# Rotated queries transposed one iteration later in a four-stage fused kernel

## Chip, cores and metric

The kernel runs on one core of a Trainium2 chip. The metric is the time of one execution on the device in microseconds (us), the median of the runs.

## What is computed

Four residual layers over x of 64 batches x 64 tokens x 512 features (float32), each with its own choice of weights per batch or per block:

```
x = x + L0(x)   # einsum('bsi,bio->bso', x, W[id]) + b[id]     16 experts, one per batch
x = x + L1(x)   # x @ W.T + low-rank adapter (A[idx], Bm[idx]) * scaling[idx], 8 adapters
x = x + L2(x)   # attention with a paged key/value cache:
                #   q, k, v = x @ Wq.T, x @ Wk.T, x @ Wv.T     8 query heads, 4 key/value heads of 64
                #   q, k = rope(rms(q)), rope(rms(k))
                #   new k, v are written into blocks; each query sees a window of 256 keys
                #   out = softmax(q k / 16) v @ Wo.T
x = x + L3(x)   # einsum('bct,bcd->bdt', x, weights[subject]) + bias[subject]
```

## The kernel before

The program is written engine by engine, with semaphores between them. Two batches (128 tokens) form a pair; there are NP = 32 pairs. **Phase one** goes over the pairs and does L0, L1, the projections of L2 and the rotation of queries and keys; the results (x2, the rotated queries, new key/value rows) go to DRAM. **Phase two** goes over the 64 batches and does attention, the output projection and L3. The change lies in phase one alone.

Each engine has its own function `phase_one(k, j, s)` for iteration k. The helper `loop` runs k = 0 to 3 written out, k = 4 to 29 in a hardware loop of two iterations a turn (s = 0 for even k, s = 1 for odd k), and the last ones written out. What an engine does in iteration k belongs to several pairs, since the work of a pair is spread over iterations. `on(k, lag, NP)` says whether the pair k - lag exists. In iteration k

- PE (TensorE) does, in this order: the experts of pair k (`experts`, L602), the transpositions of x2 of pair k-1 (`transpose_x2`, L612), the transpositions of rotated queries of pair k-2 (`transpose_queries`, L677), the transpositions of x1 of pair k (L706), the projections of pair k-1 to queries, keys and values (`project_inputs`, L654 to L666, with the adapter L623 in between), the dense part of L1 for pair k (L728, L732);
- ACT (ScalarE) copies and rounds x2 (x2t_hi, L919), copies the transposed queries into q_t (`copy_queries`, L905), copies x1 (L926, L927), and later stores q_t to DRAM (`store_queries`, L910) and squares the projections (L963, L964);
- DVE (VectorE) adds the experts' result to x (x1, L1200), forms the low parts (L1205, L1234), the sums for the norm (ss, L1257, L1259), the products of the rotation (L1265 to L1268) and x2 (L1276);
- POOL (GpSimd) does the rotation of pair k-2: the power for the norm (rms, L471), the sum (L475), the scaled rotated queries (q_rot, L480), the same for the keys (L482, L485), and the tables (L494) and x plus bias (L461) of later pairs;
- SP issues the loads, two iterations ahead, and stores.

`q_rot` and `q_t` have two buffers, one for even and one for odd pairs. POOL overwrites a buffer of q_rot once its old pair has been transposed (semaphore t3_done); PE waits for POOL (rot_q_ready) and for ACT's copy out of its PSUM bank (qt_ready). On each engine the order of the code is the order of execution; a wait holds all that stands behind it on that engine.

In the last iterations the order differs. In k = 31 (NP-1) three transpositions of index rows stand ahead of L677. In k = 32 (NP) PE has no experts; it transposes x2 of pair 31, projects it (L639), transposes the queries of pair 30 behind that, and keeps its clock up with transpositions whose result isn't used (`keep_warm`, L579). In k = 33 the queries of pair 31, which DVE has rotated (L1183), are transposed.

Of the kernel before, what the change touches and what calls it, by code (L numbers as in the profile page):

```python
# [13 lines left out]
P = 128  # L14
# [45 lines left out]
def build(nc, a):  # L60

    ctx = ExitStack()
    with ctx:
# [195 lines left out]
        def wait(eng, semaphore, value):  # L259

            if not isinstance(value, int) or value > 0:
                eng.wait_ge(semaphore, value)
# [312 lines left out]
        def _(pe):  # L575
# [90 lines left out]
                            last = nc.tensor.matmul(ps_out[:, :], x2t_hi[:, c, :], wqkv_lo[:, c, n0:n0 + D], start=False, stop=(c == DC - 1))  # L666
                    last.then_inc(qkv_done, 1)

            def transpose_queries(k, s):

                if isinstance(k, int) and k == NP + 1:
                    pe.wait_ge(q_last, 1)
                else:
                    pe.wait_ge(rot_q_ready, k - 1)
                wait(pe, qt_ready, k - 2)
                for c in range(DC):
                    last = nc.tensor.transpose(ps_t3[:, c * P:(c + 1) * P], q_rot[:, s, c * P:(c + 1) * P], ident[:, :])  # L677
                last.then_inc(t3_done, 1)

            def phase_one(k, j, s):  # L680
                r = 1 - s
                if isinstance(k, int) and k == 1:
                    transpose_x2(k, r)
                    project_inputs(k, s)
                    experts(k, j, s)
                else:
                    if on(k, 0, NP):
                        experts(k, j, s)
                    if on(k, 1, NP):
                        transpose_x2(k, r)  # L690
                if isinstance(k, int) and k == NP - 1:
# [3 lines left out]
                    for c in range(2):  # L695
                        nc.tensor.transpose(ps_la[:, (1 + c) * P:(2 + c) * P], rows[0][:, c:WIN:PAIR], ident[:, :])
                    nc.tensor.transpose(ps_la[:, P + WIN:], rows[0][:, WIN:WIN + P], ident[:, :]).then_inc(idx_t, 1)
                if on(k, 2, NP) and not (isinstance(k, int) and k == NP):
                    transpose_queries(k, s)
                if on(k, 0, NP):  # L700
                    pe.wait_ge(x1_ready, k + 1)
                    wait(pe, x1hi_ready, k)
# [7 lines left out]
                if not (isinstance(k, int) and k == 1):  # L710
                    project_inputs(k, s)
                if isinstance(k, int) and k == NP:
                    transpose_queries(k, s)
                    pe.wait_ge(x1_ready, NP)
                    keep_warm(WARM_Q)
                if on(k, 0, NP):

                    if isinstance(k, int) and k < 2:
                        adapt_down(k, s)
                    wait(pe, x2_ready, k)  # L720
                    if isinstance(k, int) and k == 0:
                        pe.wait_ge(w_hi_ready, 1)
                        pe.wait_ge(w1_lo_ready, 1)
                    pe.wait_ge(x1hi_ready, k + 1)
                    pe.wait_ge(x1lo_ready, k + 1)
                    for x_part, w_part in ((x1t_hi, w1_hi), (x1t_hi, w1_lo), (x1t_lo, w1_hi)):
                        for c in range(DC):
                            nc.tensor.matmul(ps_l1[:, :], x_part[:, c, :], w_part[:, c, :],  # L728
                                             start=(c == 0 and x_part is x1t_hi and w_part is w1_hi), stop=False)
                    pe.wait_ge(xa_ready, k + 1)  # L730
                    pe.wait_ge(pb_ready, k + 1)
                    nc.tensor.matmul(ps_l1[:, :], xa_parts[:, :], pair_b_parts[:, s, :], start=False, stop=True).then_inc(h_done, 1)  # L732
# [135 lines left out]
        def _(act):  # L868
# [29 lines left out]
            for k in range(2):  # L898
                take_adapters(k, k, copy=False)

            def copy_queries(k, j, s):

                act.wait_ge(t3_done, k - 1)
                wait(act, st_q[s], 16 * j - 16)
                nc.scalar.activation(q_t[:, s, :, :, :], ps_t3[:, :].rearrange("p (c h t) -> p h c t", c=DC, h=2),  # L905
                                     ACT.Copy).then_inc(qt_ready, 1)

            def store_queries(k, s):
                act.wait_ge(qt_ready, k - 1)
                act.dma_start(q_dram[bass.ds(k - 2, 1)].rearrange("o p n -> (o p) n"),  # L910
                              q_t[:, s, :, :, :].rearrange("p h c t -> p (h c t)")).then_inc(st_q[s], 16)

            def phase_one(k, j, s):
                r = 1 - s
                if on(k, 1, NP):

                    act.wait_ge(t2_done, k)
                    wait(act, qkv_done, k - 1)
                    nc.scalar.activation(x2t_hi[:, :, :].rearrange("p c t -> p (c t)"), ps_t2[:, :], ACT.Copy).then_inc(x2hi_ready, 1)  # L919
                if on(k, 2, NP) and not (isinstance(k, int) and k == NP):  # L920
                    copy_queries(k, j, s)
                if on(k, 0, NP):

                    act.wait_ge(t1_done, k + 1)
# [18 lines left out]
                if isinstance(k, int) and k == 0:  # L943
                    act.wait_ge(ld_wkv, 2 * 16)
                    nc.scalar.activation(wqkv_hi[:, :, D:], wqkv_stage[:, :, D:], ACT.Copy).then_inc(w_hi_ready, 1)
                if on(k, 2, NP) and not (isinstance(k, int) and k == NP):
                    store_queries(k, s)
                if isinstance(k, int) and k == NP:

                    act.wait_ge(kv_done, 1)  # L950
# [3 lines left out]
                    nc.scalar.activation(kv_out[:, r, 256:512], ps_kv[:, 256:512], ACT.Copy).then_inc(v_ready, 1)  # L954
                    act.wait_ge(qkv_done, k)
                    nc.scalar.activation(sq[:, 0:8, :].rearrange("p g d -> p (g d)"), ps_q[:, :], ACT.Square).then_inc(sqv_ready, 1)
                    copy_queries(k, j, s)
                    store_queries(k, s)
                elif on(k, 1, NP):

                    act.wait_ge(qkv_done, k)
# [474 lines left out]
```

## Time and profile before

| | |
|---|---|
| runs | 950.08, 950.8, 954.0 us; median 950.8 |
| profiled execution | span 948.6 us (its time outside the span isn't recorded) |
| mean granted clock of PE | 0.982 |
| busy | PE 96%, PE weight loads 70%, DVE 69%, POOL 55%, ACT 47% of the span |
| phase one | up to about 500 us: 32 iterations, most of them of 14.6 to 14.7 us |
| turn to phase two | about 500 to 530 us |
| phase two | from there to the end |

Times in the rows are in us from the start of the span, durations of single instructions too. PE's matmuls are pipelined: a group's busy time holds the way of the last one through the array, so the start of one group and the start of the next tell more than its end. PEld is the weight load that belongs to a matmul or transposition.

### The profile page before, as it was taken

What the parts mean: (1) busy time and instruction counts of PE and PEld (TensorE: products, weight loads), DVE (VectorE), ACT (ScalarE), POOL (GpSimd) and SP (SyncE); (2) the same over time, 40 slices, a digit from 0 to 9 for tenths busy, and PEclk for the clock granted to TensorE, in tenths of its full rate; (3) what the DMA queues carried; (4) which work ended last, traced back from release to release, by engine and by line L of the source; (5) the groups of instructions that cost most, each with busy time, mean ns of one, the idle gap of its engine ahead of it and who ended that gap; (6) DMA issues with size and microseconds to landing.
All of it is one profiled execution on the core that took longest, in us unless ns stands there. A gap on an engine that the chain in (4) does not pass through costs nothing.

```text
span 948.6 us, 23332 instructions
## 1 busy us (share of the span) xinstructions
PE 907.5 (96%) x6477; PEld 660.8 (70%) x6477; DVE 651.1 (69%) x1853; ACT 444.3 (47%) x1190; POOL 522.3 (55%) x502
## 2 busy tenths in 40 slices
PE   5789999999999999999997899999999999999997
PEld 3456666766666667666676777877777887787785
DVE  5345545667768774556754678777878877888875
ACT  2333333333333333333322566666666666666663
POOL 2136455464564657855556666566565665656530
PEclk9799999999999999999998799999999999999999
DMA  9978988778788787887844566666666676567741
GB/s 295 265 230 282 330 308 290 252 261 289 247 282 276 244 291 255 271 295 247 284 159 152 183 188 203 199 210 186 198 197 212 200 225 203 181 209 212 221 135 46
DMA packets 100413, 218.51 MB, mean 230 GB/s; under 512 B 30187, under 2 KB 36168, under 8 KB 92178
## 3 DMA queue, kind: packets, MB, share of 16 engines
q1 hardware_dynamic: 66290, 145.27, 47.0%
q0 software_dynamic: 25088, 57.74, 20.5%
q10 hardware_dynamic: 8992, 15.00, 4.9%
q8 instruction: 18, 0.29, 0.1%
q14 instruction: 25, 0.20, 0.1%
HBM read 210.39 MB, written 33.86 MB: 257 GB/s over the span
## 4 chain that ended last, share of the span: by engine, by line
PE 51%; POOL 18%; issue 15%; DMA 7%; SPq 4%; DVE 2%; ACT 1%; ACTq 1%; POOLq 0%; DVEq 0%
PE banks L823 9%; PE banks L775 9%; PE banks L811 7%; PE banks L798 6%; POOL rms L471 5%; DMA ring<-in_rope 5%; PE banks L752 4%; PE banks L859 3%; POOL ring L475 3%; POOL x_in L461 3%; PE banks L816 3%; POOL q_rot L480 2%; PE banks L753 1%; PE banks L791 1%; POOL ring L482 1%
## 5 line engine op out<-in xcount | busy, mean ns | idle before, releaser
L561 POOL DMA_INDIRECT ring<-new_rows,idx x128 | 129.4, 1011 | 82.5 <-PE banks L775 40.3
L471 POOL TENSOR_TENSOR rms<-ss,neg_half 128x12 f32<-128x12 f32 x31 | 70.8, 2284 | 185.4 <-DVE ss L1259 185.4
L992 ACT ACTIVATE big<-big,neg_max 128x320 f32<-128x320 f32 x256 | 141.4, 554 | 3.1 <-DVE neg_max L1317 2.7
L1317 DVE CUSTOM_DVE_ANT_0 big<-banks,mask 128x320 f32<-128x320 f32 x256 | 114.6, 486 | 27.4 <-PE banks L775 26.0
L602 PE MATMUL banks<-ring 128*64 128x512 f32 x512 | 117.8, 601 | 0.9 <-DMA ring<-in_w 0.9
L982 ACT ACTIVATE kt<-banks 128x384 f32<-128x384 f32 x128 | 61.8, 483 | 97.5 <-PE banks L753 97.5
L775 PE MATMUL banks<-kt,q_in 64*128 64x128 f32 (+2 forms) x768 | 88.6, 364 | 1.3 <-ACT kt L982 1.3
L550 POOL DMA_INDIRECT ring<-new_rows,idx x64 | 61.7, 965 | 47.0 <-PE banks L798 42.7
L1354 DVE TENSOR_SCALAR big<-big,recip 128x320 f32<-128x320 f32 x256 | 85.5, 396 | 2.3
L775 PEld LDWEIGHTS banks<-kt,q_in 64*128 64x128 f32 x768 | 74.4, 189 | 14.4 <-issue 8.4
L811 PEld LDWEIGHTS banks<-pt,ring 128*64 128x64 f32 x1024 | 55.4, 136 | 38.1 <-DVE pt L1299 25.4
L602 PEld LDWEIGHTS banks<-ring 128*64 128x64 f32 x512 | 34.1, 137 | 67.6 <-issue 66.8
L919 ACT ACTIVATE x2t_hi<-banks 128x512 fp32r<-128x512 f32 x32 | 19.1, 598 | 128.0 <-PE banks L612 128.0
L514 POOL DMA_INDIRECT ring<-in_kvrows,idx x64 | 61.2, 956 | 28.8 <-issue 13.5
L811 PE MATMUL banks<-pt,ring 128*64 128x128 f32 x1024 | 70.0, 278 | 2.7 <-DVE pt L1299 2.3
L664 PE MATMUL banks<-wqkv_hi,x2t_lo 128*128 128x512 f32 x248 | 70.4, 405 | 0.0
L798 PE MATMUL banks<-ident,big 128*128 128x128 f32 x512 | 67.4, 275 | 0.4 <-DVE ot_lo L1306 0.4
L654 PE MATMUL banks<-wqkv_hi,x2t_hi 128*128 128x512 f32 x248 | 66.6, 412 | 0.7 <-ACT x2t_hi L919 0.7
L666 PE MATMUL banks<-wqkv_lo,x2t_hi 128*128 128x512 f32 x248 | 66.6, 390 | 0.0
L1234 DVE TENSOR_TENSOR x1t_lo<-x1t,x1t_hi 128x512 fp32r<-128x512 f32 x32 | 40.3, 1258 | 35.9 <-ACT x1t L927 35.9
L1200 DVE TENSOR_TENSOR x<-banks,x_in 128x512 f32<-128x512 f32 x32 | 22.1, 691 | 55.6 <-PE banks L602 50.9
L798 PEld LDWEIGHTS banks<-ident,big 128*128 128x128 f32 x512 | 58.5, 142 | 1.0 <-DVE ot_lo L1306 0.9
(177 smaller groups left out, 1989.0 us busy)
## 6 DMA issues: line engine op xcount, KB each, us to landing
ring<-in_w SPq DMA_DIRECT2D x62, 1024.0 KB, 7.5
ring<-in_xt SPq DMA_DIRECT2D x32, 256.0 KB, 2.7
x_in<-in_x SPq DMA_DIRECT2D x32, 256.0 KB, 5.8
bias_in<-in_b SPq DMA_DIRECT2D x64, 128.0 KB, 6.4
x_dram<-x SPq DMA_DIRECT2D x32, 256.0 KB, 6.9
q_dram<-q_t ACTq DMA_DIRECT2D x32, 256.0 KB, 5.7
new_rows<-kv_out SPq DMA_DIRECT2D x32, 256.0 KB, 6.7
q_in<-q_dram SPq DMA_DIRECT2D x32, 256.0 KB, 2.7
```

The source lines that it names most:

```text
L471: nc.gpsimd.tensor_tensor(rms[:, s, :], ss[:, s, :], neg_half[:, :], ALU.pow).then_inc(rms_ready, 1)
L561: pool.indirect_dma_start(out=kv[:, s, c, :], out_offset=None, in_=new_rows, in_offset=bass.IndirectOffsetOnAxis(ap=idx[:, b, 1 + c:2 + c] ...
L602: last = nc.tensor.matmul(ps_l0[T * h:T * h + T, :], xt[:, s, c, T * h:T * h + T], w0[:, 2 * s + h, c * D:(c + 1) * D], start=(c == 0), st ...
L654: nc.tensor.matmul(ps_out[:, :], x2t_hi[:, c, :], wqkv_hi[:, c, n0:n0 + D], start=(c == 0), stop=False)
L664: nc.tensor.matmul(ps_out[:, :], x2t_lo[:, c, :], wqkv_hi[:, c, n0:n0 + D], start=False, stop=False)
L775: return nc.tensor.matmul(banks[:, S0[g] + n0:S0[g] + n1], q_in[r0:r0 + HD, s % 4, g // 2, :], kt[r0:r0 + HD, s % 2, g // 2, k0 + n0:k0 + ...
L798: last = nc.tensor.transpose(ps_pt[p][:, (q * 2 + c) * P:(q * 2 + c + 1) * P], prob[:, r % 2, (5 * p + 3 * q + c) * P:(5 * p + 3 * q + c + ...
L811: nc.tensor.matmul(ps_o[p][HD * q:HD * q + HD, :], kv[:, r, c, v0:v0 + HD], pt[:, p, PLACE[2 * p + q] % 2, c, :], start=(c == 0), stop=Fal ...
L823: last = nc.tensor.matmul(out[:, n0:n1], o_part[:, pair_s, c, :], w_part[:, c, n0:n1], start=(c == 0 and n == 0), stop=(c == DC - 1 and n ...
L992: nc.scalar.activation(prob[:, s % 2, PLACE[g] * NK:(PLACE[g] + 1) * NK], sm[:, s % 2, g, :], ACT.Exp, bias=neg_max[:, s % 2, g:g + 1], sc ...
L1317: V.tensor_tensor_reduce(sm[:, s % 2, g, :], ps_s[g], mask[:, s % 2, k0:k0 + NK], 1.0, 3.0e38, ALU.add, ALU.min, accum_out=neg_max[:, s % ...
L1354: V.tensor_scalar(own_row, own_row, recip[:, s % 2, g:g + 1], None, ALU.mult).then_inc(prob_ready, 1)
```

## The change

The rotated queries of pair k-3, not k-2, are transposed in iteration k, at the same place of PE's order. The copies and stores on ACT move along. The functions now take the pair and its buffer as arguments. Where the pairs run out, in k = 32, the queries of pair 29 are transposed ahead of x2 and copied ahead of x2t_hi; pairs 30 and 31 stay where they were.

```diff
-            def transpose_queries(k, s):
-                if isinstance(k, int) and k == NP + 1:
+            def transpose_queries(pair, t):
+                if is_last(pair):
                     pe.wait_ge(q_last, 1)
                 else:
-                    pe.wait_ge(rot_q_ready, k - 1)
-                wait(pe, qt_ready, k - 2)
+                    pe.wait_ge(rot_q_ready, pair + 1)
+                wait(pe, qt_ready, pair)
                 for c in range(DC):
-                    last = nc.tensor.transpose(ps_t3[:, c * P:(c + 1) * P], q_rot[:, s, c * P:(c + 1) * P], ident[:, :])
+                    last = nc.tensor.transpose(ps_t3[:, c * P:(c + 1) * P], q_rot[:, t, c * P:(c + 1) * P], ident[:, :])
...
                     if on(k, 0, NP):
                         experts(k, j, s)
+                    if isinstance(k, int) and k == NP:
+                        transpose_queries(NP - 3, r)
                     if on(k, 1, NP):
                         transpose_x2(k, r)
...
-                if on(k, 2, NP) and not (isinstance(k, int) and k == NP):
-                    transpose_queries(k, s)
+                if on(k, 3, NP) and on(k, 0, NP):
+                    transpose_queries(k - 3, r)
...
                 if isinstance(k, int) and k == NP:
-                    transpose_queries(k, s)
+                    transpose_queries(NP - 2, s)
                     pe.wait_ge(x1_ready, NP)
                     keep_warm(WARM_Q)
+                if isinstance(k, int) and k == NP + 1:
+                    transpose_queries(NP - 1, s)
...
-            def copy_queries(k, j, s):
-                act.wait_ge(t3_done, k - 1)
-                wait(act, st_q[s], 16 * j - 16)
+            def copy_queries(pair, half, t):
+                act.wait_ge(t3_done, pair + 1)
+                wait(act, st_q[t], 16 * half)
...
+                if isinstance(k, int) and k == NP:
+                    copy_queries(NP - 3, NP // 2 - 2, r)
                 if on(k, 1, NP):
                     act.wait_ge(t2_done, k)
...
-                if on(k, 2, NP) and not (isinstance(k, int) and k == NP):
-                    copy_queries(k, j, s)
+                if on(k, 3, NP) and on(k, 0, NP):
+                    copy_queries(k - 3, j - 2 + s, r)
+                if isinstance(k, int) and k == NP + 1:
+                    copy_queries(NP - 1, NP // 2 - 1, s)
...
-                if on(k, 2, NP) and not (isinstance(k, int) and k == NP):
-                    store_queries(k, s)
+                if on(k, 3, NP) and on(k, 0, NP):
+                    store_queries(k - 3, r)
+                if isinstance(k, int) and k == NP:
+                    store_queries(NP - 3, r)
+                if isinstance(k, int) and k == NP + 1:
+                    store_queries(NP - 1, s)
```

The order on PE in the even half of the loop, from the experts to the projections; before (`ident` is the unit matrix that a transposition multiplies with, a name in brackets is the semaphore waited for):

```order
L612 MATMUL banks<-ident,x2 128x128 [waits x2lo_ready]
L612 MATMUL banks<-ident,x2 128x128 x3
L262 REGISTER_ALU [waits rot_q_ready]
L677 MATMUL banks<-ident,q_rot 128x128 [waits qt_ready]
L677 MATMUL banks<-ident,q_rot 128x128 x3
L701 REGISTER_ALU
L706 MATMUL banks<-ident,x1 128x128 [waits x1hi_ready,x1_ready]
L706 MATMUL banks<-ident,x1 128x128 x3
L654 MATMUL banks<-wqkv_hi,x2t_hi 128x512 [waits sqv_ready,ab_ready,x2hi_ready]
```

The same place with the change:

```order
L612 MATMUL banks<-ident,x2 128x128 [waits x2lo_ready]
L612 MATMUL banks<-ident,x2 128x128 x3
L674 REGISTER_ALU
L262 REGISTER_ALU [waits rot_q_ready]
L677 MATMUL banks<-ident,q_rot 128x128 [waits qt_ready]
L677 MATMUL banks<-ident,q_rot 128x128 x3
L703 REGISTER_ALU
L708 MATMUL banks<-ident,x1 128x128 [waits x1hi_ready,x1_ready]
L708 MATMUL banks<-ident,x1 128x128 x3
L654 MATMUL banks<-wqkv_hi,x2t_hi 128x512 [waits sqv_ready,ab_ready,x2hi_ready]
```

Nothing changes its place; one register instruction (L674) is added ahead of L677, and what L677 reads and the count that it waits for are those of the pair before. In the odd half, and in the iterations that are written out, no register instruction is added there.

ACT in k = 32 and behind it, before:

```order
L919 ACTIVATE x2t_hi<-banks 128x512 [waits qkv_done,t2_done]
L952 ACTIVATE sq<-banks 128x256 [waits ss_ready,kv_done]
L954 ACTIVATE kv_out<-banks 128x256 [waits st_kv1]
L956 ACTIVATE sq<-banks 128x512 [waits qkv_done]
L905 ACTIVATE q_t<-banks 128x512 [waits st_q0,t3_done]
L910 DMA q_dram<-q_t 128x512 [waits qt_ready]
```

The same with the change:

```order
L909 ACTIVATE q_t<-banks 128x512 [waits st_q1,t3_done]
L925 ACTIVATE x2t_hi<-banks 128x512 [waits qkv_done,t2_done]
L914 DMA q_dram<-q_t 128x512 [waits qt_ready]
L964 ACTIVATE sq<-banks 128x256 [waits ss_ready,kv_done]
L966 ACTIVATE kv_out<-banks 128x256 [waits st_kv1]
L968 ACTIVATE sq<-banks 128x512 [waits qkv_done]
L909 ACTIVATE q_t<-banks 128x512 [waits st_q0,t3_done]
L914 DMA q_dram<-q_t 128x512 [waits qt_ready]
```

A copy (L909) is added ahead of x2t_hi, and its store (L914) behind it. On PE four transpositions are added ahead of L612 of this iteration.

## Rows read from the trace of the kernel before

**Rows 1.** The page, the chain that ended last: share of the span by engine.

```profile
PE 51%; POOL 18%; issue 15%; DMA 7%; SPq 4%; DVE 2%; ACT 1%; ACTq 1%; POOLq 0%; DVEq 0%
```

**Rows 2.** Waits of PE's weight loads: who waited for whom: us, times, longest.

```profile
PEld banks L677 <- POOL q_rot L480: 5.5, 15, 0.8
PEld banks L677 <- issue: 4.9, 13, 0.5
```

**Rows 3.** Waits of PE's matmuls.

```profile
PE banks L602 <- DMA ring<-in_w: 0.9, 2, 0.5
```

**Rows 4.** Waits of POOL.

```profile
POOL rms L471 <- DVE ss L1259: 185.4, 31, 13.3
```

**Rows 5.** Stretch k = 3 to 29: length, busy time by engine, granted clock, DMA share.

```profile
76.32:457.26 380.94, 377.70 (x2108) 250.75 (x2107) 246.26 (x517) 134.18 (x286) 219.95 (x196) 1.00 0.85 276
```

**Rows 6.** Timeline of k = 15: start, us, engine, line, operation [idle before <- releaser].

```profile
252.02 1.04 POOL L480 TENSOR_TENSOR q_rot<-ring,rms 128x512 f32<-128x512 f32 x1
252.26 0.42 PEld L612 LDWEIGHTS banks<-ident,x 128*128 128x128 f32 x4 [0.81 <-issue]
...
252.38 0.69 DVE L1200 TENSOR_TENSOR x<-banks,x_in 128x512 f32<-128x512 f32 x1 [1.33 <-PE banks L602]
252.95 0.60 ACT L919 ACTIVATE x2t_hi<-banks 128x512 fp32r<-128x512 f32 x1 [3.92 <-PE banks L612]
...
253.11 0.42 PEld L677 LDWEIGHTS banks<-ident,q_rot 128*128 128x128 f32 x4 [0.44 <-POOL q_rot L480]
...
253.50 0.47 PEld L706 LDWEIGHTS banks<-ident,x 128*128 128x128 f32 x4
...
253.94 1.69 PEld L654 LDWEIGHTS banks<-wqkv_hi,x2t_hi 128*128 128x128 f32 x8
```

**Rows 7.** Timeline of k = 16.

```profile
264.93 0.68 DVE L1276 TENSOR_TENSOR x<-banks,x 128x512 f32<-128x512 f32 x1
...
266.57 1.04 POOL L480 TENSOR_TENSOR q_rot<-ring,rms 128x512 f32<-128x512 f32 x1
266.98 0.42 PEld L612 LDWEIGHTS banks<-ident,x 128*128 128x128 f32 x4 [0.81 <-issue]
...
267.74 0.42 PEld L677 LDWEIGHTS banks<-ident,q_rot 128*128 128x128 f32 x4 [0.33 <-issue]
...
267.76 0.60 ACT L919 ACTIVATE x2t_hi<-banks 128x512 fp32r<-128x512 f32 x1 [3.97 <-PE banks L612]
...
268.56 1.70 PEld L654 LDWEIGHTS banks<-wqkv_hi,x2t_hi 128*128 128x128 f32 x8
```

**Rows 8.** Timeline, L612 and L654 of k = 3, 29 and 30.

```profile
76.32 0.42 PEld L612 LDWEIGHTS banks<-ident,x 128*128 128x128 f32 x4 [0.81 <-issue]
...
77.84 0.77 PEld L654 LDWEIGHTS banks<-wqkv_hi,x2t_hi 128*128 128x128 f32 x4
...
457.26 0.42 PEld L612 LDWEIGHTS banks<-ident,x 128*128 128x128 f32 x4 [0.81 <-DVE x L1276]
...
459.29 0.30 PEld L654 LDWEIGHTS banks<-wqkv_hi,x2t_hi 128*128 128x128 f32 x2
...
472.34 0.42 PEld L612 LDWEIGHTS banks<-ident,x 128*128 128x128 f32 x4 [0.81 <-issue]
...
473.85 0.53 PEld L654 LDWEIGHTS banks<-wqkv_hi,x2t_hi 128*128 128x128 f32 x3
```

**Rows 9.** Timeline of k = 32, the turn to phase two.

```profile
500.24 0.65 PE L612 MATMUL banks<-ident,x 128*128 128x128 f32 x4 [2.20 <-DVE x L1276]
500.93 0.60 ACT L919 ACTIVATE x2t_hi<-banks 128x512 fp32r<-128x512 f32 x1 [4.65 <-PE banks L612]
...
501.58 1.79 PE L639 MATMUL banks<-wqkv_hi,x2t_hi 128*128 128x512 f32 x4 [0.69 <-ACT x2t_hi L919]
```

**Rows 10.** Two stretches of the turn: columns as in rows 5.

```profile
501.50:505.00 3.50, 3.42 (x9) 2.70 (x10) 0.69 (x1) 0.03 (x1) 2.04 (x3) 0.56 0.27 103
...
513.26:533.00 19.74, 16.18 (x82) 13.63 (x82) 8.64 (x30) 6.64 (x19) 14.43 (x15) 0.65 0.59 176
```

More of the change, by code:

```diff
@@ L899, in _, with store_queries @@
                 take_adapters(k, k, copy=False)
-            def copy_queries(k, j, s):
-                act.wait_ge(t3_done, k - 1)
-                wait(act, st_q[s], 16 * j - 16)
-                nc.scalar.activation(q_t[:, s, :, :, :], ps_t3[:, :].rearrange("p (c h t) -> p h c t", c=DC, h=2),
+            def copy_queries(pair, half, t):
+                act.wait_ge(t3_done, pair + 1)
+                wait(act, st_q[t], 16 * half)
+                nc.scalar.activation(q_t[:, t, :, :, :], ps_t3[:, :].rearrange("p (c h t) -> p h c t", c=DC, h=2),
                                      ACT.Copy).then_inc(qt_ready, 1)
[L908 to L911, printed above, removed]
+            def store_queries(pair, t):
+                act.wait_ge(qt_ready, pair + 1)
+                act.dma_start(q_dram[bass.ds(pair, 1)].rearrange("o p n -> (o p) n"),
+                              q_t[:, t, :, :, :].rearrange("p h c t -> p (h c t)")).then_inc(st_q[t], 16)
             def phase_one(k, j, s):
                 r = 1 - s
+                if isinstance(k, int) and k == NP:
+                    copy_queries(NP - 3, NP // 2 - 2, r)
                 if on(k, 1, NP):
@@ L956, in phase_one @@
                     nc.scalar.activation(sq[:, 0:8, :].rearrange("p g d -> p (g d)"), ps_q[:, :], ACT.Square).then_inc(sqv_ready, 1)
-                    copy_queries(k, j, s)
-                    store_queries(k, s)
+                    copy_queries(NP - 2, NP // 2 - 1, s)
+                    store_queries(NP - 2, s)
                 elif on(k, 1, NP):
```

## The prediction

> **What bounds the kernel now.** I began with the chain that ended last, because it says which engine to follow: PE holds 51% of it and POOL 18% [rows 1]. POOL's share is the rotation of queries and keys in phase one, and the change touches the place where that work is handed to PE. So the next view was the list of PE's waits, for the weight loads alone, since a load starts when a transposition is released. The transpositions of rotated queries (L677) stood 5.5 us behind POOL's q_rot in 15 iterations and 4.9 us, listed as "issue", in 13 more [rows 2]. That is one wait in each of the 28 iterations k = 3 to 30. The loop takes 14.65 us an iteration: from the start of L612 in k = 3 to that in k = 29 there are 26 periods in 380.94 us, at a granted clock of 1.00 throughout and with PE busy for 377.70 us of it [rows 5]. PE is therefore the bound of phase one, and each stop of PE lengthens the iteration unless something else is late behind it.
>
> Two other candidates fall out. The expert weights held PE for 0.9 us in the whole run [rows 3]. POOL stood 185.4 us idle before its first rotation step, waiting in all 31 cases for DVE's sums [rows 4], and those come out of PE's projections; so POOL follows PE and doesn't pace it.
>
> **One iteration.** In k = 15 [rows 6] PE starts the transpositions of x2 (L612) at 252.26 and has loaded them at 252.68. POOL finishes q_rot at 252.02 + 1.04 = 253.06; L677 starts at 253.11. Behind it in PE's order come the transpositions of x1 (L706, 253.50) and the projections (L654, 253.94). L654 stands 1.68 us after L612. In k = 16 the same steps give 266.98 and 268.56, so 1.58 us [rows 7], with q_rot at 267.61 and L677 at 267.74. The rest of the iteration, from L654 to the next L612, has no stop of PE of this kind; what shortens the stretch from L612 to L654 shortens the period.
>
> **The change, part by part.** It removes no instruction from a full iteration. PE's order in the loop is the same, L612, L677, L706, L654, but L677 now takes the pair that POOL rotated a whole iteration earlier. POOL's L480 of k = 15 ends at 253.06 and the L677 that will read it now stands near 267.4, some 14 us behind. The wait of rows 2 is gone, 10.4 us in all.
>
> *What is late next.* Three things release L654 after L612. First PE's own flow: the four loads of L612 take 0.42, L677 to L706 0.39, L706 to L654 0.44, together 1.25 us [rows 6]. Second DVE's x1: L1200 starts 0.12 after L612 and takes 0.69, so x1 is there at 0.81; L706 at about 0.87, and L654 0.44 later at 1.31. Third ACT's x2t_hi: L919 starts 0.69 after L612 in k = 15 and 0.78 in k = 16, since it has to wait for L612's results, and takes 0.60; that is 1.29 and 1.38. After an end of L919 at 501.53 PE's next instruction started at 501.58 [rows 9], so 0.05 for the hand-over. The third is the latest: L654 can't start before 1.34 us in odd iterations, nor before 1.43 in even ones. So ACT takes the place of POOL as the one PE waits for, with a shorter wait.
>
> *The sum.* Read for each of the 28 iterations, L654 now starts after L612: in the 13 odd ones k = 3 to 27 1.58 us on average (the first, k = 3, 1.52 [rows 8]); in the 13 even ones k = 4 to 28 1.62 (k = 16, 1.58 [rows 7]); in k = 29 2.03, where POOL's rotation started late; in k = 30, the last, 1.51 [rows 8]. Against 1.34 and 1.43 this is 13 x 0.24 + 13 x 0.19 + 0.69 + 0.17 = 6.4 us. The grouped rows give nearly the same: 10.4 us of waits, less what the new wait takes back, 1.34 - 1.25 = 0.09 in the 14 odd iterations and in k = 30, and 1.43 - 1.25 = 0.18 in the 13 even ones, 3.7 together; that leaves 6.7. I take 6.4, the one from single iterations.
>
> *Register instructions.* In the loop's even half PE gets one more register instruction ahead of L677, and ACT one ahead of its copy. No row shows one alone. The nearest: with the wait on POOL live, L677 started 0.05 after q_rot in k = 15, where no register instruction carries the wait, and 0.13 in k = 16, where one does [rows 6, 7], so 0.08. Between nothing and 0.08 I take nothing, because PE's own flow of 1.25 + 0.08 = 1.33 stays under the 1.43 that ACT sets there. The hand-over of ACT to L654 could also cost 0.13 instead of 0.05; on 28 iterations that is 2.2 us and leaves 4.2. I take 0.05, since no register instruction stands ahead of L654 in the order.
>
> *Iteration 2 and the turn to phase two.* Iteration 2 loses its L677, but there PE waits for x1 anyway; nothing. In k = 31 L677 didn't wait before; nothing. In k = 32 four transpositions are added ahead of L612. PE stood idle 2.20 us there, for DVE's x2 [rows 9], and four transpositions are 0.42, so they are hidden. On ACT the copy of that pair (0.60) now stands ahead of L919, which had been idle 4.65 us [rows 9]; hidden too. The store of pair 29 is issued one iteration later than before, but still ahead of that of pair 30, whose copy follows the last projections; phase two waits for both, and pair 30's is the later. If the 2.20 us of cover were gone, the transpositions and the copy would cost about 0.42 + 0.60 = 1.0 once.
>
> POOL's rewriting of a q_rot buffer waits for its transposition. That now comes one iteration later, but still about 13 us ahead of the rewriting: L677 near 253, the next L480 at 266.57. No cost. DVE's x2 for the next L612 was ready at 265.61 against 266.98 [rows 7]: 1.37 us to spare.
>
> **The rivals.**
>
> *The clock at the turn.* After the 2.20 us of idle PE the stretch 501.5 to 505 ran at a granted 0.56 [rows 10], so for most of it at the lower of the two levels, 1.2 GHz, and the first four matmuls of it took 1.79 us [rows 9]. Were the clock kept up there, the same work would need 3.5 x 0.56 = 2.0 us, so 1.5 less. The added transpositions put work into this gap; yet 1.8 us of it remain. The Trainium skill, TensorE: Matmul & The Clock Gate, Part 1 (the HAM clock gate), says that the throttled state is the default and activity releases it; by that the clock might hold. The trace agrees that idling and the fall stand together, but no run here shows that four transpositions suffice. With this gain 944.4 - 1.5 = 942.9.
>
> *Dearer hand-overs.* L654's release costs 0.13 rather than 0.05, or x1 comes late by as much. The gain is 4.2 to 4.7, the time 946.1 to 946.6. For it: x1 and x2t_hi lie within 0.1 us of each other as limits. Against it: the order of instructions ahead of L654 isn't changed.
>
> *Another engine sets the period.* If the loop through DVE's sums, POOL and the loads paced phase one, an earlier L654 would be given back as a wait elsewhere: no gain, 950.8. For it: 18% of the chain on POOL [rows 1], a DMA share of 0.85 in the loop [rows 5]. Against it: rows 3 and 4.
>
> *Slower.* From 513.26 to 533.00 PE ran at a granted 0.65 [rows 10], which at the cost of 0.35 x 19.74 us is already 6.9 us of PE's time. Where the low stretches lie depends on where PE's idle times fall, and the change moves them. Each us at half clock beyond the present ones costs 0.5 us at PE's pace. To lose the 6.4 and another 4.8, some 22 us more at the lower level are needed, as much as rows 10 show in all. The time would be 955.6 or more. Against it: from 533 on nothing that PE waits for is changed.
>
> That the change does nothing isn't a case: every iteration from 3 on takes another buffer and another count in its waits.
>
> **How the numbers follow.** The span of 948.6 us becomes 942.2. The runs lie 1.5 to 5.4 above that span, their median 950.8 is 2.2 above it; the profiled execution's own time outside its span isn't shown. I set the same 2.2 on top: 944.4. Chances: forecast 0.56 (944.1 to 946.0), clock kept 0.10 (942.9), dearer hand-overs 0.20 (946.1 to 946.6), another engine 0.10 (950.8), slower 0.04. A measurement of this kernel tells about 0.5%, 4.8 us, from no change; 946.0 is that edge. Faster is 0.56 + 0.10 = 0.66; the same 0.20 + 0.10 = 0.30; slower 0.04. The range takes the first three cases, 0.86 together, and the 0.9 us by which the runs' lowest lies under their median at the lower end: 942.0; at the upper end 946.6 and about as much of drift, with part of the fourth case: 948.5.
>
> **What would show it right or wrong.** Right: L677 follows L612 by 0.39 to 0.42 in every iteration; no wait of L677 on q_rot in the loop; L654 1.34 and 1.43 after L612, released by x2t_hi; period 14.65 - 0.24 = 14.4. Wrong in the hand-over: L654 at 1.5. Wrong in the bound: L654 early, and a new wait at L612, L602 or L732, with the period still 14.6. The turn: L612 of k = 32 still released by DVE's x2, and a granted clock after it that is either still 0.56 or 1.00.

## The result, and the profile after

The changed kernel takes 943.52 us (median of four runs, 942.83 to 944.91) where the kernel before takes 950.83 (four runs). The ratio on record is 0.9911, interval 0.9885 to 0.9936; the quotient of the two medians, 0.9923, lies inside it. The forecast was 944.4. The profiled execution took 943.37 us with a span of 941.6, against 948.6 before, at a mean granted clock of 0.989 against 0.982.

The chain that ended last, by engine, of the kernel after, answers [rows 1]:

```profile
PE 91%; DMA 3%; DVE 2%; issue 2%; ACT 1%; SPq 1%; ACTq 0%; POOL 0%; DVEq 0%; POOLq 0%
```

POOL's 18% are gone, and so is most of "issue" (15% to 2%); PE's share of the chain went from 51% to 91%. The waits of PE's weight loads after (who waited for whom, us in total, times, longest), which answer [rows 2]:

```profile
PEld banks L708 <- DVE x L1212: 6.4, 6, 3.1
...
PEld banks L677 <- DVE q_rot L1195: 1.5, 1, 1.5
...
PEld banks L654 <- ACT x2t_hi L925: 1.1, 1, 1.1
```

Both rows of L677 behind POOL (5.5 us in 15 places, 4.9 us in 13) have no successor. The one wait on q_rot that is left is that for the last pair, whose q_rot DVE makes. Some lines have moved down: L925 is L919 of before (x2t_hi), L708 is L706 (transpositions of x1), L1212 is L1200 (DVE's x1).

The timeline of k = 15 after (start, us, engine, line, operation, tiles), to be read beside [rows 6]:

```profile
252.00 1.05 POOL L480 TENSOR_TENSOR q_rot<-ring,rms 128x512 f32<-128x512 f32 x1
252.03 0.42 PEld L612 LDWEIGHTS banks<-ident,x 128*128 128x128 f32 x4 [0.81 <-issue]
...
252.15 0.69 DVE L1212 TENSOR_TENSOR x<-banks,x_in 128x512 f32<-128x512 f32 x1 [1.12 <-PE banks L602]
252.41 0.47 PEld L677 LDWEIGHTS banks<-ident,q_rot 128*128 128x128 f32 x4
...
252.72 0.60 ACT L925 ACTIVATE x2t_hi<-banks 128x512 fp32r<-128x512 f32 x1 [3.56 <-PE banks L612]
252.89 0.43 PEld L708 LDWEIGHTS banks<-ident,x 128*128 128x128 f32 x4
...
253.37 0.30 PEld L654 LDWEIGHTS banks<-wqkv_hi,x2t_hi 128*128 128x128 f32 x2
```

POOL's q_rot still ends at 253.05, as late as before, but L677 starts at 252.41, 0.38 after L612, with no idle time listed. L654 comes 1.34 after L612 (1.68 before). ACT's x2t_hi ends at 253.32 and L654 starts 0.05 later: this is the new last release. The list of waits doesn't show it: there L654 stands behind x2t_hi once only, so here the release is read from the times, and e7 and e8 below try it. k = 16 after, beside [rows 7]:

```profile
266.42 0.42 PEld L612 LDWEIGHTS banks<-ident,x 128*128 128x128 f32 x4 [0.81 <-issue]
...
267.20 0.60 ACT L925 ACTIVATE x2t_hi<-banks 128x512 fp32r<-128x512 f32 x1 [3.42 <-PE banks L612]
...
267.85 0.30 PEld L654 LDWEIGHTS banks<-wqkv_hi,x2t_hi 128*128 128x128 f32 x2
```

Here it is 1.43 (1.58 before), again 0.05 behind x2t_hi's end at 267.80. In k = 29, where late q_rot had drawn the stretch from L612 to L654 out to 2.03 us [rows 8], POOL is no earlier: its L480 starts 0.31 after L612 (0.11 before). PE no longer sees it (1.35):

```profile
454.02 0.42 PEld L612 LDWEIGHTS banks<-ident,x 128*128 128x128 f32 x4 [0.81 <-DVE x L1288]
...
454.33 1.05 POOL L480 TENSOR_TENSOR q_rot<-ring,rms 128x512 f32<-128x512 f32 x1
...
455.37 0.30 PEld L654 LDWEIGHTS banks<-wqkv_hi,x2t_hi 128*128 128x128 f32 x2
```

**Where the span went.** Stretches of both kernels (from and to; length, busy time of PE, PEld, DVE, ACT and POOL with their instructions, granted clock of TensorE, DMA share, GB/s). The cuts are the start of L612 in k = 3 and in k = 32, then 13 us and 20 us behind it, then the end. First before:

```profile
76.32:500.24 423.92, 417.90 (x2338) 278.99 (x2337) 274.61 (x578) 147.22 (x314) 245.18 (x220) 1.00 0.82 269
500.24:513.24 13.00, 11.07 (x56) 9.10 (x56) 6.38 (x17) 4.25 (x6) 6.71 (x8) 0.87 0.27 101
513.24:533.24 20.00, 16.23 (x84) 13.71 (x85) 8.81 (x31) 6.88 (x19) 14.69 (x15) 0.66 0.59 176
500.24:948.60 448.36, 435.33 (x3876) 346.49 (x3876) 340.72 (x1174) 275.59 (x839) 254.68 (x259) 0.98 0.61 187
```

and after:

```profile
78.98:496.14 417.16, 415.42 (x2342) 280.45 (x2340) 275.80 (x578) 144.78 (x315) 248.53 (x220) 1.00 0.84 273
496.14:509.14 13.00, 10.26 (x61) 8.52 (x62) 7.95 (x19) 4.85 (x7) 8.27 (x9) 0.99 0.39 130
509.14:529.14 20.00, 14.31 (x115) 12.02 (x116) 8.24 (x32) 8.32 (x25) 14.22 (x14) 0.92 0.64 197
496.14:941.60 445.46, 429.73 (x3876) 342.00 (x3876) 340.75 (x1174) 276.61 (x839) 254.63 (x259) 1.00 0.63 188
```

The span lost 7.0 us in three parts: the loop 6.76 (423.92 to 417.16), the rest behind it, the tail, 2.90 (448.36 to 445.46), while the start grew by 2.66 (76.32 to 78.98). The loop is what the forecast was about. The other two all but cancel, yet each is large enough for a second effect, and the tail looks like the rival in which the clock is kept at the turn: granted 0.99 in place of 0.87 over the 13 us there, and 0.92 in place of 0.66 in the next 20. One profile of each kernel can't tell that from chance, so both became questions for the runs.

### The profile page after: what moved, and what is told of

Same layout as the page of the kernel before. It is cut to its first block, busy times and chain, and to the rows that moved or that the text cites. A ratio compares the mean times of both kernels' runs of the same rounds, so it can differ in the third digit from the quotient of the medians.

```text
span 941.6 us, 23372 instructions
## 1 busy us (share of the span) xinstructions
PE 900.2 (96%) x6477; PEld 658.3 (70%) x6477; DVE 651.8 (69%) x1853; ACT 442.4 (47%) x1190; POOL 525.5 (56%) x502
## 4 chain that ended last, share of the span: by engine, by line
PE 91%; DMA 3%; DVE 2%; issue 2%; ACT 1%; SPq 1%; ACTq 0%; POOL 0%; DVEq 0%; POOLq 0%
PE banks L602 12%; PE banks L827 9%; PE banks L732 9%; PE banks L779 9%; PE banks L815 7%; PE banks L664 7%; PE banks L654 7%; PE banks L666 6%; PE banks L802 6%; PE banks L756 4%; PE banks L863 3%; PE banks L820 3%; PE banks L623 2%; PE banks L612 2%; PE banks L708 2%
## 5 line engine op out<-in xcount | busy, mean ns | idle before, releaser
L779 PE MATMUL banks<-kt,q_in 64*128 64x128 f32 (+2 forms) x768 | 86.7, 358 | 1.3 <-ACT kt L994 1.3
L925 ACT ACTIVATE x2t_hi<-banks 128x512 fp32r<-128x512 f32 x32 | 19.1, 598 | 118.8 <-PE banks L612 118.8
L654 PE MATMUL banks<-wqkv_hi,x2t_hi 128*128 128x512 f32 x248 | 67.8, 417 | 0.7 <-ACT x2t_hi L925 0.7
L461 POOL TENSOR_TENSOR x_in<-x_in,bias_in 128x512 f32<-128x512 f32 x32 | 48.1, 1503 | 22.5 <-DMA ring<-in_rope 15.8
L1212 DVE TENSOR_TENSOR x<-banks,x_in 128x512 f32<-128x512 f32 x32 | 22.1, 692 | 55.2 <-PE banks L602 49.2
```

The source lines that it names most:

```text
L654: nc.tensor.matmul(ps_out[:, :], x2t_hi[:, c, :], wqkv_hi[:, c, n0:n0 + D], start=(c == 0), stop=False)
L779: return nc.tensor.matmul(banks[:, S0[g] + n0:S0[g] + n1], q_in[r0:r0 + HD, s % 4, g // 2, :], kt[r0:r0 + HD, s % 2, g // 2, k0 + n0:k0 + ...
```

## The experiments

The theory, A: PE waited for POOL's q_rot in 28 iterations; ACT's x2t_hi is the next release of L654 and now sets the stretch. A2 adds that the four transpositions put into the gap at the turn keep the clock up. The rivals: another engine, POOL before all, sets the period (C), or the gains at the turn and the losses at the start are where low stretches of the clock happen to fall. The runs were made in three groups, each on another chip, where the kernel before had medians of 952.61, 951.49 and 952.74 us over 17 runs each; the ratios are to these, but for the first result, whose four runs of the kernel before had 950.83.

| kernel | us, runs | ratio, interval | start | loop | tail | clock in 13 us |
|---|---|---|---|---|---|---|
| before | 950.83, 4 | | 76.32 | 423.92 | 448.36 | 0.87 |
| after | 943.52, 4 | 0.9911, 0.9885 to 0.9936 | 78.98 | 417.16 | 445.46 | 0.99 |
| e1_before_again | 953.24, 12 | 1.0007, 0.9985 to 1.0029 | 80.47 | 424.16 | 448.87 | 0.87 |
| e2_second_gap_filled | 944.20, 6 | 0.9920, 0.9891 to 0.9950 | 80.22 | 417.09 | 444.99 | 1.00 |
| e3_turn_behind | 945.66, 6 | 0.9928, 0.9902 to 0.9955 | 76.72 | 417.17 | 447.81 | 0.87 |
| e4_both_gaps_filled | 944.08, 6 | 0.9909, 0.9878 to 0.9939 | 79.03 | 417.18 | 444.59 | 1.00 |
| e5_rotation_late_before | 974.26, 4 | 1.0220, 1.0182 to 1.0257 | 83.86 | 443.68 | 447.76 | 0.74 |
| e6_rotation_late_after | 946.71, 10 | 0.9938, 0.9917 to 0.9958 | 79.71 | 416.86 | 446.33 | 0.87 |
| e7_copy_in_halves | 942.23, 6 | 0.9899, 0.9873 to 0.9925 | 76.16 | 414.38 | 446.46 | 0.87 |
| e8_copy_ahead | 971.44, 4 | 1.0210, 1.0175 to 1.0244 | 77.72 | 444.34 | 447.54 | 0.87 |
| a1_after_again | 945.74, 6 | 0.9934, 0.9915 to 0.9953 | 78.34 | 416.90 | 448.06 | 0.87 |
| e11_turn_behind_again | 944.46, 6 | 0.9918, 0.9902 to 0.9934 | 79.28 | 416.90 | 444.82 | 1.00 |
| e10_before_turn_filled | 952.08, 12 | 0.9988, 0.9976 to 0.9999 | 79.72 | 424.45 | 447.63 | 1.00 |
| e9_halves_turn_filled | 944.38, 5 | 0.9916, 0.9902 to 0.9931 | 78.28 | 414.38 | 447.24 | 1.00 |

Start, loop and tail are those of the stretches above, of the one profile of each kernel; the times are medians of all its runs.

### Is the loop's gain the wait for POOL?

One operation of POOL was added ahead of the sum that q_rot is made from, once to the kernel before (e5_rotation_late_before) and once to the kernel after (e6_rotation_late_after). Its result goes nowhere. The lines of both shift by two: L679 is L677, L614 is L612.

```diff
+                    nc.gpsimd.tensor_tensor(spare[:, :, :], rot_a[:, 0:4, :], rot_b[:, 0:4, :], ALU.add)
                     nc.gpsimd.tensor_tensor(rot[:, 0:8, :], rot_a[:, 0:8, :], rot_b[:, 0:8, :], ALU.add).then_inc(rot_q_sum, 1)
```

> The kernel before with one more POOL instruction (128x256, 0.73 us) ahead of the sum that q_rot is made from, in each of 31 iterations; its result isn't used. Theory A (PE waits for q_rot in each of 28 iterations): every one of these waits grows by 0.73 us, and k = 31 begins to wait by about 0.6; 950.8 + 28 x 0.73 + 0.6 = 971.9 us. Rival C (another engine sets the period and the wait on q_rot is filled by it): less than half of that, under 961.

> The changed kernel with the same additional POOL instruction. Theory A: q_rot is used a whole iteration later, so nothing waits: 943.5 us give or take 1. Rival C (POOL's loop is the next bound): up to 0.73 us an iteration, 943.5 + 20 = 964.

The added operation in e6 (POOL's groups by line: busy us, mean ns), then the loop of e5 and that of e6 (columns as above):

```profile
L476 POOL TENSOR_TENSOR spare<-ring 128x256 f32<-128x256 f32 x31 | 22.8, 736 | 0.0
```

```profile
83.86:527.54 443.68, 418.14 (x2338) 278.94 (x2336) 273.72 (x578) 147.19 (x314) 262.89 (x249) 1.00 0.78 256
```

```profile
79.71:496.57 416.86, 415.11 (x2342) 280.50 (x2341) 283.19 (x578) 144.88 (x315) 276.45 (x249) 1.00 0.86 272
```

The same 0.74 us of POOL in each iteration costs the kernel before 443.68 - 423.92 = 19.8 us of its loop, 0.68 in each of the 28 iterations that waited and 0.60 in k = 31, which now waits too, and the kernel after nothing (416.86 against 417.16). The time of e5, 974.26, is 2.4 above the 971.9 that was expected, though the loop gave 19.8 where 21.0 was expected; the rest lies outside the loop (its start is at 83.86). In e5 PE's waits for q_rot grew by about as much:

```profile
PEld banks L679 <- POOL q_rot L482: 17.8, 17, 1.5
PEld banks L679 <- issue: 13.8, 13, 1.1
```

That is 31.6 us where [rows 2] has 10.4. So POOL's time stood on the path before and has left it. The rival in which another engine sets the period asked for a loop near 424 in the kernel after; the loop stays at 416.9 with POOL made slower still, so it falls. The time of e6, 946.71, is above the 943.5 give or take 1 that was expected; its loop isn't the reason, and its ratio lies within the interval of a1, the kernel after run again.

### Is ACT's copy the new release?

e8_copy_ahead puts ACT's copy of the rotated queries ahead of x2t_hi in the loop; e7_copy_in_halves splits x2t_hi, so that PE may start on its first half.

```diff
+                if on(k, 3, NP) and on(k, 0, NP):
+                    copy_queries(k - 3, j - 2 + s, r)
                     act.wait_ge(t2_done, k)
                     wait(act, qkv_done, k - 1)
                     nc.scalar.activation(x2t_hi[:, :, :].rearrange("p c t -> p (c t)"), ps_t2[:, :], ACT.Copy).then_inc(x2hi_ready, 1)
-                if on(k, 3, NP) and on(k, 0, NP):
-                    copy_queries(k - 3, j - 2 + s, r)
```

> The changed kernel with ACT's copy of the transposed queries ahead of x2t_hi in every iteration from 3 to 31. The copy can start about 1.15 us after L612 and takes 0.6, x2t_hi ends at about 2.3. Theory A: L654 comes about 2.35 us after L612, 0.9 to 1.0 later in 29 iterations: 943.5 + 26 to 29 = 970 to 972. Rival D (x2t_hi isn't the limit): less than half of that.

Loop and PE's wait in e8:

```profile
77.72:522.06 444.34, 420.46 (x2342) 280.54 (x2340) 269.06 (x578) 144.73 (x315) 242.71 (x220) 1.00 0.76 256
```

```profile
PEld banks L654 <- ACT x2t_hi L927: 30.2, 30, 1.1
```

The loop is 27.2 us longer than after's, 0.94 in each of its 29 iterations (k = 3 to 31), and the trace names the place: L654 waits for x2t_hi in 30 places, 30.2 us in all, and comes 2.27 after L612 in odd and 2.36 in even iterations, where 2.35 was expected. There is no slack behind that copy.

```diff
-                    nc.scalar.activation(x2t_hi[:, :, :].rearrange("p c t -> p (c t)"), ps_t2[:, :], ACT.Copy).then_inc(x2hi_ready, 1)
+                    for n in range(2):
+                        nc.scalar.activation(x2t_hi[:, 2 * n:2 * n + 2, :].rearrange("p c t -> p (c t)"), ps_t2[:, 256 * n:256 * n + 256],
+                                             ACT.Copy).then_inc(x2hi_ready, 1)
...
-                    pe.wait_ge(x2hi_ready, k)
+                    pe.wait_ge(x2hi_ready, 2 * k - 1)
...
+                            if c == 2 and n0 == 0:
+                                pe.wait_ge(x2hi_ready, 2 * k)
```

> The changed kernel with ACT's x2t_hi in two halves of 128x256, each with its own signal, and L654 waiting for the second only ahead of its third chunk. Theory A (x2t_hi is what PE waits for now, 0.05 and 0.13 us beyond x1 and PE's own flow): L654 comes 1.30 to 1.32 us after L612 in odd and even iterations, the period falls by 0.04 and 0.12, 2 us in all: 941.5. Rival D (PE's own flow or x1 is already the limit): L654 stays at 1.34 and 1.43, 943.5. DVE's low part waits for both halves, which end about 0.15 us later.

Timeline of k = 15 in e7 (L656 is L654, L710 the x1 transpositions, L1216 DVE's x1, L928 ACT's halves):

```profile
248.30 0.42 PEld L612 LDWEIGHTS banks<-ident,x 128*128 128x128 f32 x4 [0.81 <-DVE x L1292]
...
248.42 0.69 DVE L1216 TENSOR_TENSOR x<-banks,x_in 128x512 f32<-128x512 f32 x1 [0.80 <-PE banks L602]
...
248.99 0.66 ACT L928 ACTIVATE x2t_hi<-banks 128x256 fp32r<-128x256 f32 x2 [3.29 <-PE banks L612]
249.16 0.43 PEld L710 LDWEIGHTS banks<-ident,x 128*128 128x128 f32 x4
...
249.56 0.30 PEld L656 LDWEIGHTS banks<-wqkv_hi,x2t_hi 128*128 128x128 f32 x2
```

L656 comes 1.26 after L612 in all odd and in ten of the 13 even iterations, where the kernel after has 1.34 and 1.43. In k = 4, 6 and 8 it comes 1.40 to 1.42 after, and L710 at 1.02 to 1.03, because DVE's x1 is late there. The loop shrinks by 2.8 us to 414.38, a little more than the 2 expected. So freeing x2t_hi earlier pays, which is the other side of e8, and the next limit lies at 1.26 in most iterations: L710 stands 0.05 behind the end of DVE's x1 (249.11), and L656 0.40 behind L710. PE's own flow gives 1.25 [rows 6]; but for k = 4, 6 and 8, where it is x1, the two can't be told apart here. This is the shortest loop of all the kernels, but its interval, 0.9873 to 0.9925, overlaps both of the kernel after, so its gain over it is shown by the trace of the loop and not by the times.

### Are start and turn worth something?

e1_before_again is the kernel before and a1_after_again the kernel after, unchanged. They show what one kernel does from execution to execution.

> The kernel before, unchanged, for a second profile and the scatter of its runs. Theory A (the wait on POOL's rotation is the loop's gain, and PE's two idle gaps, in iteration 2 and at the turn, add or take 2 to 3 us through the clock that follows them): 950 to 951.5 us, L654 again 1.5 to 1.7 us after L612, a granted clock of 1.00 after the gap of iteration 2 and below 0.9 after the gap of 2.20 us at the turn. Rival B (start and turn scatter by chance in every kernel): the same time, but start and turn differ from the first profile by 2 us or more.

> The changed kernel, unchanged, for a second profile and the scatter of its runs beside the next three. Theory A (the loop gains 6.8 us from iteration 3 to 32 and the rest of the difference is chance of start and turn): from L612 of iteration 3 to that of iteration 32 again 417.2 us, the ratio to the kernel before 0.9925 give or take 0.0025, that is about 944 to 945 where before gives 951.5. Theory A2 (the four transpositions in the gap of the turn are worth another 2 us through the clock): the end lies 445 to 446.5 us behind L612 of iteration 32, where the kernel before had 448.3 and 448.9.

Of e1 the start of L612 in k = 3 lies at 80.47 instead of 76.32, with the same loop:

```profile
80.47:504.63 424.16, 417.83 (x2338) 279.00 (x2337) 271.65 (x578) 147.20 (x314) 244.47 (x220) 1.00 0.82 268
```

A start that moves by 4.2 us with nothing changed gives no ground to call the 2.66 of the kernel after a cost of the change. The largest part of it lies in iteration 2, from its L612 to the next; before, after, e1 and a1 in this order:

```profile
59.82:76.32 16.50, 14.54 (x83) 9.65 (x82) 8.29 (x25) 5.16 (x11) 8.00 (x8) 1.00 0.82 272
60.40:78.98 18.58, 15.71 (x79) 10.37 (x78) 8.30 (x25) 4.67 (x10) 8.46 (x9) 0.91 0.76 243
61.89:80.47 18.58, 16.13 (x83) 10.78 (x81) 8.30 (x25) 5.16 (x11) 8.47 (x9) 0.91 0.79 252
61.86:78.34 16.48, 14.10 (x79) 9.21 (x77) 8.30 (x25) 4.67 (x10) 8.01 (x8) 1.00 0.84 277
```

It takes 16.5 us at a granted 1.00 and 18.6 at 0.91, and each kernel shows both. The turn of e1 is that of the first profile (0.87, tail 448.87). Of a1:

```profile
78.34:495.24 416.90, 415.14 (x2342) 280.69 (x2340) 277.63 (x578) 144.79 (x315) 245.68 (x220) 1.00 0.83 273
495.24:508.24 13.00, 11.08 (x56) 9.11 (x56) 6.37 (x17) 4.26 (x6) 7.03 (x8) 0.87 0.32 119
495.24:943.30 448.06, 431.06 (x3876) 342.76 (x3876) 341.06 (x1174) 276.35 (x839) 254.21 (x259) 0.99 0.62 187
```

The loop repeats to 0.3 us. The turn of the kernel after doesn't: the same program with the same four transpositions in the gap now has a granted 0.87 over the 13 us, as the kernel before, and a tail of 448.06.

e3_turn_behind and e11_turn_behind_again are one kernel run in two groups. It moves the transpositions of pair 29, and their copy, from ahead of x2's in k = 32 to behind them, so that the gap stands empty as before.

```diff
-                    if isinstance(k, int) and k == NP:
-                        transpose_queries(NP - 3, r)
                     if on(k, 1, NP):
                         transpose_x2(k, r)
+                    if isinstance(k, int) and k == NP:
+                        transpose_queries(NP - 3, r)
```

> The changed kernel with the transpositions of pair 29 in iteration 32 behind those of x2 instead of ahead of them, and their copy on ACT behind x2t_hi; so the idle gap of PE there is 2.2 us again instead of 1.75. Theory A: the clock falls behind the gap as in the kernel before, 0.56 instead of 0.99 in the stretch after it, and the time is 945.0 to 946.4 us. Rival B: the clock at the turn is chance, the time is 943.5 give or take 0.7.

> The changed kernel with the transpositions of pair 29 behind those of x2 in iteration 32, a second time, beside the changed kernel itself. Theory A2: 1.5 to 2.5 us more than the changed kernel of the same call, the end 447.5 to 449 behind L612 of iteration 32. Theory A (chance): the same time within 1 us.

The 13 us and the tail, of e3 and then of e11:

```profile
493.89:506.89 13.00, 11.53 (x60) 9.54 (x60) 6.36 (x16) 4.74 (x7) 6.89 (x8) 0.87 0.34 126
493.89:941.70 447.81, 433.15 (x3880) 344.64 (x3880) 340.89 (x1174) 277.09 (x840) 254.93 (x259) 0.99 0.61 188
```

```profile
496.18:509.18 13.00, 10.70 (x66) 9.01 (x67) 7.99 (x19) 5.34 (x8) 8.29 (x9) 1.00 0.40 139
496.18:941.00 444.82, 430.13 (x3880) 342.60 (x3880) 341.10 (x1174) 276.85 (x840) 254.31 (x259) 1.00 0.61 189
```

e3 alone looked like a proof of A2: without the transpositions in the gap the clock falls and the tail is 2.4 us longer than after's. Run again, the same kernel keeps 1.00 with the gap empty, and its tail is shorter than after's; its median, 944.46, is below the 945.74 of a1 beside it, where A2 asked for 1.5 to 2.5 more. With a1 that makes all four combinations: gap with transpositions and kept clock (after), with them and fallen (a1), without them and fallen (e3), without them and kept (e11). Of all profiles without further filling, 0.99 or more is kept in two of the six with the four transpositions in the gap (after, e2) and in one of the five without (e11). Four transpositions don't decide it; A2 falls.

Three kernels fill the gap with transpositions of the identity, whose result goes nowhere. e10_before_turn_filled does so in the kernel before:

```diff
+                    if isinstance(k, int) and k == NP:
+                        pe.wait_ge(x1_ready, NP)
+                        keep_warm(18)
                     if on(k, 1, NP):
                         transpose_x2(k, r)
```

> The kernel before with 18 transpositions whose result isn't used ahead of L612 of iteration 32, and nothing else; the loop is the old one. Theory A2: no low stretch of the clock behind this gap, the end 444.6 to 446 behind L612 of iteration 32, time 2 to 3 us under the kernel before. Theory A (chance): the kernel before's time within 1 us.

```profile
504.17:517.17 13.00, 10.27 (x62) 8.57 (x63) 8.00 (x19) 4.85 (x7) 7.99 (x9) 1.00 0.31 109
517.17:537.17 20.00, 15.50 (x94) 12.84 (x93) 7.16 (x28) 7.05 (x20) 13.88 (x15) 0.66 0.62 176
504.17:951.80 447.63, 433.02 (x3876) 344.45 (x3876) 340.69 (x1174) 275.70 (x839) 254.71 (x259) 0.98 0.62 187
```

A full gap holds the clock at 1.00 right behind it, but the next 20 us stay at the 0.66 that the kernel before has there. The tail is 0.7 us shorter than before's, where A2 asked for 444.6 to 446; the time is 0.9988 of before's, which by the interval is 0.1 to 2.3 us. So a clock forced to stay up at this place is worth 0.7 us by the two tails and at most 2.3 by the times, not the 2.9 of the first pair of profiles.

e9_halves_turn_filled is e7 with 14 such transpositions, e2_second_gap_filled puts 16 behind x2's transpositions in k = 2, and e4_both_gaps_filled has e2's 16 and 14 at the turn, both on the kernel after. The part that e2 and e4 share:

```diff
                     if on(k, 1, NP):
                         transpose_x2(k, r)
+                    if isinstance(k, int) and k == 2:
+                        for _ in range(16):
+                            nc.tensor.transpose(ps_t3[:, 0:P], ident[:, :], ident[:, :])
```

> The changed kernel with x2t_hi in halves and 14 unused transpositions ahead of L612 of iteration 32. From L612 of iteration 3 to that of iteration 32 414.4 us as in the kernel with halves alone, 2.8 under the changed kernel. Theory A2: behind that 444.6 us, so 3.5 to 4 us under the changed kernel. Theory A: 2.8 under it.

> The changed kernel with 16 transpositions whose result isn't used behind L612 of iteration 2, where the change took four away. Theory A: the clock doesn't fall behind this gap, the start of L612 in iteration 3 lies about 16.5 us behind that of iteration 2 instead of 18.6, and the time is 941.4 us, 2.1 less than the changed kernel's 943.5. Rival B: the fall was chance, the time is 943.5.

> The changed kernel with 16 unused transpositions behind L612 of iteration 2 and 14 more ahead of L612 of iteration 32. Theory A: no low stretch behind either gap, 941.4 us or up to 1 us less. Rival B: 943.5.

With e9 the loop is e7's 414.38 to the hundredth and the clock 1.00 over the 13 us, yet its tail is 447.24, not the 444.6 of A2, and its ratio, 0.9916, is no better than e7's 0.9899. Iteration 2 takes 19.61 us in e2, at a granted 0.91, and 17.01 in e4, at 1.00, where A expected about 16.5; their starts, 80.22 and 79.03, are later than after's 78.98. So the work put into k = 2 doesn't keep the clock up for certain, nor bring an early start back. Their ratios of 0.9920 and 0.9909 lie around after's 0.9911. Filling either gap shows no gain in the times.

**What stays open.** Over all profiles the tail is 447.6 to 448.9 us in the four kernels with the old order (mean 448.2) and 444.6 to 448.1 in the ten with the new (mean 446.3). A small gain behind the loop may therefore be there. The medians leave little room for it: the seven results with the loop of the kernel after (the first one, e2, e3, e4, e6, a1, e11) lie 4.8 to 8.5 us under the kernel before of their group, 7.3 on average, of which the loop is about 7. No run here names a cause.

## Why the prediction was right

**The bound and the removed wait: right.** L677 on POOL was the wait of all 28 iterations [rows 2]; it is gone, and e5 against e6 shows that POOL's time up to q_rot was on the path before and isn't any more. The chain of waits pointed there, and the loop's PE share [rows 5] said that a shorter wait would pass through.

**What is late next: right, with its size.** L654 stands 1.34 after L612 in odd and 1.43 in even iterations, released by x2t_hi, with 0.05 of hand-over: the three numbers of the forecast. e8 and e7 moved this release both ways, and the loop followed by 27.2 us more and 2.8 less. The rival of dearer hand-overs asked for L654 later by 0.08 and falls. The hand-over taken from the turn [rows 9] held in the loop.

**The sum: 0.4 too small.** With the measured stretches it is 13 x (1.58 - 1.34) + 13 x (1.62 - 1.43) + (2.03 - 1.35) + (1.51 - 1.34) = 3.1 + 2.5 + 0.7 + 0.2 = 6.4 as forecast, and 6.5 when all 28 stretches are added up singly; the loop lost 6.76 in the first profile and 7.0 in a1. The 0.3 to 0.5 that are left lie between L654 and the next L612, some 0.01 to 0.02 in each iteration, and no row puts them on one place. The grouped waits gave 6.7 and were as near. Period: 26 of them took 454.02 - 78.98 = 375.04, 14.42 each, where 14.4 was forecast.

**x1 as the third limit: mis-sized.** It was put at 1.31 (x1's end, 0.05, and 0.44 from L706 to L654). In e7, where x2t_hi no longer hides it, L654 comes at 1.26; the step that was mis-sized is the 0.44, which measures 0.40 there. Nor is x1 there at 0.81 in every iteration: in k = 4, 6 and 8 of the kernel after L708 starts 1.02 to 1.04 after L612, in k = 4 with a wait for x1 of 0.18 listed, and L654 comes 0.41 later, so there x1 is as late as x2t_hi. In the other iterations it changed nothing, since x2t_hi is later than either.

**Iteration 2 and the turn.** "Nothing" for k = 2 isn't contradicted: the start is later by 2.66 in the first profile, but e1 moves it by 4.2 without any change, iteration 2 takes 16.48 us in a1, and e3 and e7, with the new order, start at 76.72 and 76.16. The four transpositions at the turn and their copy are hidden, as said. In the kernel after, PE still waits there for DVE's x2, 1.75 us where [rows 9] has 2.20:

```profile
496.15 0.66 PE L612 MATMUL banks<-ident,x 128*128 128x128 f32 x4 [1.75 <-DVE x L1288]
...
497.49 1.21 PE L639 MATMUL banks<-wqkv_hi,x2t_hi 128*128 128x512 f32 x4 [0.69 <-ACT x2t_hi L925]
```

The four matmuls of L639 took 1.21 us and not the 1.79 of before (1.61 in a1). Read alone, this looks like the rival "the clock at the turn", with the granted clock that it asked for. a1 and e11 show that it isn't tied to the transpositions, so it is no effect of the change that the runs can show.

**The time.** 944.4 was the forecast, 943.5 the first median, 0.9934 of the kernel before the repeated one. In part that is luck: start and tail, which the sum put at nothing, moved by +2.66 and -2.90 and all but cancelled, and the median lies 0.6 below the 944.1 to 946.0 that the forecast's own case was given. The overhead over the span was put at 2.2 us, from a median and the span of one run; on record it is 1.8 in each of the four runs (943.37 - 941.6 in the profiled one). At the lower end of the range, the runs' lowest lies 0.7 under their median, not 0.9. The case "slower" set 22 us at the lower level against the stretches of rows 10: these are 23 us long, but by their granted clock some 17 of it are at that level. The case "slower", more low stretches behind the loop, shows in none of the profiles of the new order: no tail of theirs is longer than before's 448.36.

## What to carry to other kernels

Where a wait sits in a loop on the engine that is the bound, the gain of removing it is not its length: list every other release of the next instruction, in microseconds from one common start, and subtract the latest. Here 10.4 us of waits gave 6.8, and the same list then showed the next step, the copy in halves, which shortened the loop by another 2.8. A difference outside the part that was changed is to be measured again on both kernels before it is explained: one profile of each had shown a mechanism at the turn that a second profile of the changed kernel took back.

## What the runs showed of the hardware

The place of the low stretches of TensorE's clock varies between executions of one program. The kernel after had a granted 0.99 in the 13 us behind the turn once and 0.87 the next time, e3's program 0.87 and then 1.00, and the tails differ by 2.6 and 3.0 us beside it; how much of that the clock makes isn't shown. In iteration 2 both kernels had 1.00 once and 0.91 once. At the turn PE's idle time ahead of L612 was the same in both executions (1.75 and 1.76 us in the kernel after, 2.19 and 2.20 in e3's program), so that idle time, on which the case "slower" of the prediction leaned, doesn't place them alone. The Trainium skill, TensorE: Matmul & The Clock Gate, Part 1 (the HAM clock gate), says of a kernel's start that the number of matmuls at the lower of the two levels differs from run to run of one kernel; the traces here show the same in the middle of one, at the turn. The same section's rule that activity releases the throttle, by which the prediction gave the clock a chance, agrees with the runs where the gap is filled: e4, e9 and e10 have 1.00 in the 13 us behind it, three of three. But e10 then runs at 0.66 in the 20 us after that, and the three tails are 444.59, 447.24 and 447.63 us.

An operation on POOL of 0.74 us costs this loop 0.68 us an iteration (e5) or nothing (e6), by whether PE reads its result in the same iteration or in the next.
